# Two graph attention layers on one core: the scaled rows of both layers in half rows that begin at multiples of 16 bytes

## The reference

```python
# layer 0: 8 heads of width 128, x is [4096, 256]
Wh = einsum('nf,hfd->hnd', x, W_heads)
e = leaky_relu(s1[:, :, None] + s2[:, None, :], 0.2)   # s1, s2: Wh with a1, a2
att = softmax(where(adj > 0, e, -9e15), axis=-1)
feat = elu(einsum('hnm,hmd->hnd', att, Wh))            # heads side by side: [4096, 1024]
x = layernorm(x + feat @ W_out + b_out)
# layer 1: 4 heads of width 64
xt = einsum('ni,hio->hno', x, W)
att = softmax(where(adj > 0, leaky_relu(src + dst, 0.2), -inf), axis=2)
x = layernorm(x + heads_side_by_side(att @ xt))
```

## Time and profile before

| | us |
|---|---|
| median of 3 runs | 2743.63 |
| lowest and highest run | 2739.69, 2745.17 |
| span of the profiled execution, first to last instruction | 2745.7 |
| setup and projections | 0 to 191 |
| layer 0's sweeps | 191 to 2045.6 |
| the stage between | 2045.6 to 2232 |
| layer 1's sweeps and the end | 2232 to 2745.7 |

### The profile page before, as it was taken

One profiled execution on the slowest core, in us unless ns is written; L12 is line 12 of the kernel. 1 busy time (PEld: TensorE's weight loads), 2 busy tenths in 40 slices (PEclk: granted clock), 3 DMA queues, 4 the chain that ended last, 5 costly groups with the idle time before them and its releaser, 6 DMA issues.

```text
span 2745.7 us, 62711 instructions
## 1 busy us (share of the span) xinstructions
PE 2674.9 (97%) x26553; PEld 2342.3 (85%) x26553; DVE 1979.0 (72%) x3206; ACT 2071.0 (75%) x3253; POOL 571.0 (21%) x479
## 2 busy tenths in 40 slices
PE   8889999999999999999999999999999999999998
PEld 6558887888888888888888888888888889999998
DVE  6546678777776776777777677675555679989898
ACT  5467877777777777777777777777763669999997
POOL 1220036333222322332322232230002310000000
PEclk9999999999999999999999999999999999999999
DMA  9975421111111110110111111002115555333330
GB/s 342 378 292 183 155 81 43 31 28 35 30 28 27 36 35 26 36 31 28 35 30 28 27 35 35 26 21 55 35 37 165 196 178 189 110 105 110 106 123 17
DMA packets 196384, 240.81 MB, mean 88 GB/s; under 512 B 14853, under 2 KB 125448, under 8 KB 196106
## 3 DMA queue, kind: packets, MB, share of 16 engines
q1 hardware_dynamic: 196106, 236.81, 26.9%
HBM read 178.91 MB, written 57.05 MB: 86 GB/s over the span
## 4 chain that ended last, share of the span: by engine, by line
PE 78%; DVE 9%; ACT 7%; DMA 3%; issue 2%; SPq 0%; POOL 0%; ACTq 0%; DVEq 0%; POOLq 0%
PE l_ps L781 59%; PE l_ps L890 10%; PE l_ps L818 4%; ACT l_arena L1019 3%; DMA l_wh<-l_arena 2%; PE l_ps L748 2%; ACT l_arena L1108 2%; DVE l_arena L1569 1%; DVE l_arena L1568 1%; PE l_ps L843 1%; PE l_ps L806 1%; DVE l_arena L1374 1%; DVE l_arena L1373 1%; DVE l_arena L1577 1%; DVE l_arena L1557 1%
## 5 line engine op out<-in xcount | busy, mean ns | idle before, releaser
L781 PE MATMUL l_ps<-l_arena 128*128 128x258 f16 x16384 | 1833.2, 273 | 7.9 <-DVE l_arena L1374 4.3
L781 PEld LDWEIGHTS l_ps<-l_arena 128*128 128x128 fp8e4 x16384 | 1591.6, 97 | 247.1 <-DVE l_arena L1374 5.7
L1019 ACT ACTIVATE l_arena<-l_arena 128x512 fp8e4<-128x512 f32 x2048 | 1281.5, 708 | 91.2 <-PE l_ps L781 89.2
L1373 DVE SCALAR_TENSOR_TENSOR l_arena<-l_arena,l_mask 128x512 uint32<-128x512 uint32 x512 | 468.1, 914 | 404.4 <-ACT l_arena L1019 401.6
L890 PE MATMUL l_ps<-l_arena 128*128 128x130 f16 x8000 | 475.5, 220 | 19.0 <-DVE l_arena L1577 8.3
L890 PEld LDWEIGHTS l_ps<-l_arena 128*128 128x128 fp8e4 x8000 | 470.0, 98 | 24.4 <-DVE l_arena L1569 19.7
L1374 DVE TENSOR_TENSOR l_arena<-l_arena,l_mask 128x512 uint32<-128x512 uint32 x512 | 488.4, 954 | 0.0
L1108 ACT ACTIVATE l_arena<-l_arena 128x1024 fp8e4<-128x1024 f32 x434 | 457.4, 1141 | 5.1 <-PE l_ps L890 4.7
L405 POOL TENSOR_TENSOR l_arena<-l_arena 128x516 f32<-128x516 f32 x119 | 155.0, 1303 | 1209.0 <-PE l_ps L781 1150.2
L1037 ACT COPY l_arena<-l_ps 128x258 f32<-128x258 f32 x256 | 93.8, 369 | 243.9 <-PE l_ps L781 243.7
L1379 DVE SCALAR_TENSOR_TENSOR l_arena<-l_ps,l_arena 128x258 f32<-128x258 f32 x256 | 117.3, 482 | 146.9 <-ACT l_arena L1037 146.8
(11 more groups left out here) (164 smaller groups left out, 1290.2 us busy)
## 6 DMA issues: line engine op xcount, KB each, us to landing
l_arena<-in_adj SPq DMA_DIRECT2D x128, 512.0 KB, 6.5
l_arena<-uv SPq DMA_DIRECT2D x125, 260.0 KB, 5.5
l_arena<-l_wh SPq DMA_DIRECT2D x64, 256.0 KB, 4.5
l_arena<-l_srow SPq DMA_DIRECT2D x64, 256.0 KB, 3.3
feat<-l_arena SPq DMA_DIRECT2D x64, 256.0 KB, 2.2
l_arena<-feat SPq DMA_DIRECT2D x32, 512.0 KB, 3.7
l_wh<-l_arena SPq DMA_DIRECT2D x64, 192.0 KB, 7.5
uv<-l_arena SPq DMA_DIRECT2D x8, 1040.0 KB, 5.1
```

The costliest lines, as they stand in the source:

```text
L781: last = nc.tensor.matmul(sums(t, m), pattern(k, m).bitcast(F8)[:, j, t * P:(t + 1) * P], uv[:, slot(h, order[k]) + j, 2 * m * W1:2 * (m + ...
L1019: ins = act.activation(pattern(k, 0).bitcast(F8)[:, j, :], s1b[q][:, :], ACT.Relu, bias=kc[:, h, jt:jt + 1], scale=STEEP, saturate=False)
L1373: dve.scalar_tensor_tensor(c, v, ONE8X4, m, ALU.bitwise_xor, ALU.bitwise_and)
```

## The change

The half rows get a pitch of their own. In layer 0 it is `WH = 264` columns or 528 bytes, in layer 1 `VH = 136` columns or 272 bytes, so that every half row starts at a multiple of 16 bytes. The 6 columns behind each half row are read by no matmul and written by none of the engines. The matmuls read as many columns as before. In layer 1 the sums of m = 1 move from column 130 to column 136 of their PSUM bank. DMAs of layer 1's scaled rows carry the gaps too: a chunk becomes 272 KB, a stored stage 1088 KB (1040 before).

`uv` grows by 1248 bytes a partition. The buffers behind it in the arena move up, those of layer 0 by 1248 bytes each but for one that moves by 1120 (`sc`, `kc` and what follows them), and so do those of layer 1, by 1120 to 1536 bytes (a few small ones by another multiple of 16). The arena grows by 1120 bytes, and the area set aside for dynamic DMA descriptors shrinks from 1024 to 256 bytes.

Every queue holds the same instructions in the same order with the same waits.

```diff
+    WH = 264
...
-        arena = s.sb("arena", [P, 96208], U8)
+        arena = s.sb("arena", [P, 97328], U8)
...
-        uv = at(0, F16, 2, (CPB + TWIN) * JC, 4 * W1)
-        bc = at(53664, U8, 1, nbuf, 2, JC * blk)
+        uv = at(0, F16, 2, (CPB + TWIN) * JC, 2 * WH)
+        bc = at(54912, U8, 1, nbuf, 2, JC * blk)
...
-        HD2, V1, W4 = H2 * D2, D2 + 1, 4 * (D2 + 1)
+        HD2, V1, VH, W4 = H2 * D2, D2 + 1, 136, 2 * 136
...
-            return uv[:, slot(h, c):slot(h, c) + JC, j * W1:(j + 1) * W1]
+            first = j // 2 * WH + j % 2 * W1
+            return uv[:, slot(h, c):slot(h, c) + JC, first:first + W1]
...
-            return ps2[:, t, m * 2 * V1:(m + 1) * 2 * V1]
+            return ps2[:, t, m * VH:m * VH + 2 * V1]
...
         def staged(j):
-            return stage[:, :, :, j * V1:j * V1 + D2]
+            first = j // 2 * VH + j % 2 * V1
+            return stage[:, :, :, first:first + D2]
...
-                                                            uv[:, slot(h, order[k]) + j, 2 * m * W1:2 * (m + 1) * W1],
+                                                            uv[:, slot(h, order[k]) + j, m * WH:m * WH + 2 * W1],
...
-                                at = jt * W4 + m * 2 * V1
+                                at = jt * W4 + m * VH
...
-                dve.tensor_scalar(part2[:, :, 2 * V1:], part2[:, :, 2 * V1:], fv.bitcast(F32)[:, c, h:h + 1], None,
+                dve.tensor_scalar(part2[:, :, VH:VH + 2 * V1], part2[:, :, VH:VH + 2 * V1], fv.bitcast(F32)[:, c, h:h + 1], None,
...
-    nc = bacc.Bacc("TRN2", target_bir_lowering=False, num_devices=1, dynamic_dma_scratch_size=1024)
+    nc = bacc.Bacc("TRN2", target_bir_lowering=False, num_devices=1, dynamic_dma_scratch_size=256)
```

More of the change, by code:

```diff
@@ L137, in at @@
             return flat_view
-        uv = at(0, F16, 2, (CPB + TWIN) * JC, 4 * W1)
-        bc = at(53664, U8, 1, nbuf, 2, JC * blk)
[L141 to L149, removed]
+        uv = at(0, F16, 2, (CPB + TWIN) * JC, 2 * WH)
+        bc = at(54912, U8, 1, nbuf, 2, JC * blk)
+        s1b = [at(71296 + q * 2048, F32, 4, blk) for q in range(2)]
+        mnb = [at(75392 + q * 512, F32, 4, D) for q in range(2)]
+        whx = [at(76416 + k * 2064, F32, 4, JC, W1) for k in range(4)]
+        tu, tv = (at(84672 + k * 2064, F32, 4, JC, W1) for k in range(2))
+        eu, ev = (at(88800 + k * 1024, F32, 4, H, NT) for k in range(2))
+        ident16 = at(90848, BF16, 2, P)
+        sc, kc = (at(91104 + k * 1024, F32, 4, H, NT) for k in range(2))
+        e1 = at(93152, F32, 4, TPB, 2 * W1)
+        zr = at(97280, F32, 4, 3, TPB)
         vt, mt, ob = e1[:, :, 0:W1], e1[:, :, W1:W1 + D], e1[:, :, 0:D]
         words = uv[:, :, :].rearrange("p c w -> p (c w)").bitcast(I32)
-        chunk, twin, RAW, PK = JC * 2 * W1, CPB * JC * 2 * W1, 4 * blk, blk
+        chunk, twin, RAW, PK = JC * WH, CPB * JC * WH, 4 * blk, blk
         raws = [words[:, at:at + RAW] for at in (twin, twin + RAW, 4 * chunk, 4 * chunk + RAW)]
@@ L165, in network @@
         slots = bc[:, :, :, :].rearrange("p k m c -> p (k m) c").bitcast(F32)
-        prod = at(75168 + 2064, F32, 4, H, D)
+        prod = at(76416 + 2064, F32, 4, H, D)
         wscore = slots[:, 0:KF, 0:2 * D + C2]
@@ L219, in network @@
         uv2 = at(0, F16, 2, 2, NT * W4)
-        bc2 = at(33280, U8, 1, nbuf2, 2, JC2 * blk2)
+        bc2 = at(34816, U8, 1, nbuf2, 2, JC2 * blk2)
         spare2 = at((G2 % 2) * NT * W4 * 2, U8, 1, 2, 2, JC2 * blk2)
[L222 to L234, removed]
@@ L235, in network @@
-        zr2, lam2, peaks2 = at(95616, F32, 4, TPB2), at(95648, F32, 4, 4), at(95664, F32, 4, H2 + 1)
-        top2, diag2 = at(95684, F32, 4, 1)[0:H2 + 1, :], at(95688, F32, 4, H2 + 1)[0:H2 + 1, :]
+        s1b2 = at(67584, F32, 4, 2, blk2)
+        z = at(76416, F32, 4, TPB2, F)
+        e2 = at(84608, F32, 4, TPB2, 2 * V1)
+        wall2 = at(88768, F32, 4, KF2, HD2 + 2 * H2)
+        st, mv = at(90880, F32, 4, TPB2, 6), at(76288, F32, 4, TPB2, 2)
+        rt, rs = at(76352, F32, 4, TPB2), at(76384, F32, 4, TPB2)
@@ new lines, in network @@
+        scol2 = at(91104, F32, 4, 2, NT * H2).rearrange("p m (t h) -> p m t h", h=H2)
+        eu2, ev2, sc2, kc2, nk, ta2, tb2 = (at(92128 + k * 512, F32, 4, H2, NT) for k in range(7))
+        kall, kt, kmax = at(95712, F32, 4, CPB, H2), at(95840, F32, 4, H2), at(96256, F32, 4, H2)
+        dk, fu1, fv1 = (at(base, F32, 4, CPB, H2) for base in (95872, 96288, 96416))
+        fu, fv = (at(base, I32, 4, CPB, H2) for base in (96000, 96128))
+        units2 = at(75776, F32, 4, P)[0:H2 + 1, :]
+        eps = at(96832, F32, 4, 1)
@@ L238, in network @@
+        zr2, lam2, peaks2 = at(96736, F32, 4, TPB2), at(96768, F32, 4, 4), at(96784, F32, 4, H2 + 1)
+        top2, diag2 = at(96804, F32, 4, 1)[0:H2 + 1, :], at(96808, F32, 4, H2 + 1)[0:H2 + 1, :]
         wo = at(0, F32, 4, KO, F)
         fin = [at(8192 + u * 4096, F32, 4, K) for u in range(2)]
-        stage = at(16640, F16, 2, H2, JC2 * W4).rearrange("p h (t w) -> p h t w", t=JC2)
-        whr = [at(24960 + w * 4096, F32, 4, JC2, HD2) for w in range(2)]
-        scaled = [s1b2[:, 1, :].rearrange("p (t c) -> p t c", t=JC2), at(85408, F32, 4, JC2, HD2)]
@@ L243, in network @@
-        ft = [at(57856 + p * 4096, F32, 4, KO, P) for p in range(2)]
-        xt2 = [at(85408 + p * 1024, F32, 4, KF2, P) for p in range(2)]
-        rows2 = [at(84384 + p * 512, F32, 4, P)[0:JC2 * H2, :] for p in range(2)]
+        stage = at(17408, F16, 2, H2, JC2 * W4).rearrange("p h (t w) -> p h t w", t=JC2)
+        whr = [at(26112 + w * 4096, F32, 4, JC2, HD2) for w in range(2)]
+        scaled = [s1b2[:, 1, :].rearrange("p (t c) -> p t c", t=JC2), at(86656, F32, 4, JC2, HD2)]
+        ft = [at(59392 + p * 4096, F32, 4, KO, P) for p in range(2)]
@@ L246, in network @@
+        xt2 = [at(86656 + p * 1024, F32, 4, KF2, P) for p in range(2)]
+        rows2 = [at(85632 + p * 512, F32, 4, P)[0:JC2 * H2, :] for p in range(2)]
         xin = [z[:, u, :] for u in range(4)]
@@ L362, in staged @@
         def staged(j):
-            return stage[:, :, :, j * V1:j * V1 + D2]
+            first = j // 2 * VH + j % 2 * V1
+            return stage[:, :, :, first:first + D2]
         def stage_one(j):
-            return stage[:, :, :, j * V1 + D2:(j + 1) * V1].rearrange("p h t a -> p h (t a)")
+            first = j // 2 * VH + j % 2 * V1
+            return stage[:, :, :, first + D2:first + V1].rearrange("p h t a -> p h (t a)")
         def turned_rows(c):
```

## The result

The changed kernel takes 2719.07 us (median of 4 runs) against 2744.4: a ratio of 0.9905, 95% interval 0.9894 to 0.9917. It is faster, by 25 us and not by 51, and lies outside the forecast range of 2682 to 2704. The profiled execution spans 2716.8 us, 28.9 less than before.

A forecast was written before the change was run, and what follows sets the result against it. PE, busy 97% of the span, was taken as the bound, with ACT and DVE also near their limit in layer 1. Layer 0 -40 and layer 1 -11 made -51 us, giving 2692.6 us against the 2743.6 median; range 2682 to 2704.

The forecast's parts named there:

- the price of an aligned matmul: Layer 0's sweeps: 12288 of 16384 matmuls start off 16 bytes and each saves 3.37 ns, 41.4 us.
- the gain would be 29 us: Layer 0's lower bound, if aligned matmuls stood 2.3 ns over their columns like the transposes; kept only for the range.
- The first blocks: Layer 0's first blocks, where a faster PE waits longer: 2 or 3 blocks may lose 0.65 us each; 1.4 us taken off.
- Layer 1's cycle: Layer 1's sweeps: 19.8 us on offer, but the cycle between ACT, DVE and PE lets only 11 us arrive.
- the forecast's split by blocks: Four layer 1 blocks: two give 0.86 us each, one about 1.1, the ACT and DVE one 0.2; 3.0 us together.
- Moved buffers: All moves are by multiples of 16 bytes, so no other operand changes its place within 16 bytes: 0 us.
- The larger DMAs: Layer 1's chunks and stored stages grow 4.6% but are fetched a block ahead: 0 us, or 2 us without that cover.
- only a part of layer 0's gain comes (29 us): Rival: layer 0 gains only 29 us, or aligned reads meet a stall; 2703 to 2720 us, 5%.
- The short distance belongs to the matmul that comes next: Rival: a matmul is cheap only when starting 4 bytes past the previous one's line; slower, to 2764 us, 3%.
- The rival by lines: Rival: price goes by 16-byte lines an operand touches, equal for all starts; time stays 2743.6 us, 4%.

The follow-up runs named there:

- 192-column run: The changed kernel with matmuls in blocks 1 to 7 of layer 0 reading and writing 192 of 258 columns; 0.9895 of the kernel before.
- moved_only: The changed kernel with buffers moved and descriptor area shrunk, but rows without gaps in both layers; 1.0002 of the kernel before.
- order_both: The kernel before, no gaps, with another order of the 8 matmuls of a chunk and tile in both layers; 2718.27 us, 0.9899 of before.
- after_again: The changed kernel measured once more, beside order_both on one chip; 2718.62 us, 0.99 of the kernel before.
- alt08: The changed kernel with layer 0's halves 536 bytes apart, row pitch 1056, so starts alternate 0 and 8 bytes past a multiple of 16; 2717 to 2721 us.
- cols256: The changed kernel with layer 0's matmuls reading 256 of 258 columns, two of the sums' columns left out; 109.2 ns a matmul.
- alt04: The changed kernel with layer 0's second half 516 bytes on, row pitch 1056, so starts alternate 0 and 4 bytes past a multiple of 16; 2728.86 us.

## Why the prediction was wrong

**The step that failed** is the price of an aligned matmul: "Each saves 112.5 - 109.2 = 3.37 ns". The sorting was right and the reading of it was not. The 109.2 ns were one of four distances in a repeating pattern, which the start of the matmul, the start of the next and the end of the last all explained equally well. I took the cheap one as the price of a uniform layout. Measured, a uniform layout has 110.0, and three of four distances of before carry a price for sharing. The cheap distance is 4 clocks over its columns beside dear ones of 12, and in the changed layout every distance is 6 over. On offer were 16384 x (111.71 - 110.0) = 28.0 us and not 41.4, and in layer 1 8192 x (58.41 - 56.70) = 14.0 and not 19.8. The number was in the text as a bound: the transposes of the earlier trace rows are pairs of aligned operands at 2.3 ns over their columns, "the gain would be 29 us". I set them aside as another operation; they were the nearer case, because they had the step between starts that the change makes.

**The first blocks** were the second miss: I gave 1.4 us for them. Of the 28.0 us on offer, blocks 9 to 63 could give 24.1 and gave 22.1: in six blocks (15, 23 and each eighth to 55) PE now also waits 0.3 us for DVE's patterns, at a time when POOL makes rows. There DVE is slow: its masking operation (L1378, 512 of them) takes 0.68 us where POOL is idle and 1.53 us in the median where POOL works during nearly all of it. Blocks 0 to 8, where 3.9 was on offer, became 1.2 us longer, for two reasons. Blocks 0 to 7 took 249.3 us in place of 249.9: in blocks 1 to 7 the chain over ACT and DVE leaves PE slack, as the 192-column run shows. Block 8 took 33.5 us in place of 31.7, because TensorE's clock fell there (see the last section). This also happens without the gaps, and the one profile of the kernel before happens not to have it, so these 1.8 us are a chance of the profiles and no cost of the change. The sign of the slack stood in the earlier trace rows, where PE waited for evacuations in 5 places: I took those waits as small losses beside PE's work, when they mark blocks that PE does not bound at all.

**Layer 1's cycle** was right where it was read, with the wrong price, but it does not hold for the blocks as I had sorted them. Rows 8 and 9 show block 11, counted from 0, and not block 10 as they say. The same block after the change, ACT in order of time:

```profile
2552.90 0.59 ACT L1126 COPY l_arena<-l_ps 128x520 f32<-128x520 f32 x1 [0.80 <-PE l_ps L894]
...
2555.95 26.11 ACT L1112 ACTIVATE l_arena<-l_arena 128x1024 fp8e4<-128x1024 f32 x25
2582.85 0.59 ACT L1126 COPY l_arena<-l_ps 128x520 f32<-128x520 f32 x1 [0.80 <-PE l_ps L894]
```

The wait before the copy was 1.40 and is 0.80. The 356 matmuls of that path at 1.71 ns saved are 0.61 us. Block 11 went from 30.56 to 29.96 us, which is this 0.61. But block 10, of the same length and kind before, gave only 0.10 (30.46), and so did blocks 6 and 14: PE saves its 0.87 us there and waits 0.77 us longer, 0.5 of it at the block's end, where it had not waited before. Block 8, which I had called ACT's and DVE's own, gave 0.5 and block 9 gave 0.9. Together blocks 8 to 11 take 122.1 us where they took 124.1. (The four blocks of the earlier trace rows add up to 124.2 us and not 124.3, which changes nothing.) So the forecast's split by blocks was wrong and its sum fared better: of 19.8 us I let 56% through; of 14.0, 7.8 came, also 56%. That the shares are the same is luck. In the profiles of the other runs with layer 1's gaps its sweeps take 497.2 to 500.3 us, most of the spread in the first block and in each second of four. No run took ACT's or DVE's work out of layer 1, so what the cycle holds back is read from the trace and not shown by a run.

**The rest.** Moved buffers at 0: right, shown by moved_only. The larger DMAs at 0: right too, since order_both has none of them and takes 2718.27 us beside after_again's 2718.62. In the profile after, a chunk of 272 KB still lands in 5.5 us, and a stored stage of 1088 KB in 5.2 (5.1 before). Of the rivals, "only a part of layer 0's gain comes (29 us)" is the one that happened, and I had given it 5%. "The short distance belongs to the matmul that comes next" had the right doubt, that the records could not tell which of two matmuls pays; its outcome, slower, did not come. The rival by lines is refuted as a forecast, since the time fell. Its premise that the count of lines (33) is the same for all four places stays true: with 33 lines each, a matmul took 264 to 268 clocks in the mean. The Trainium skill, "SBUF — State Buffer", section "Specifications (TRN2)", speaks of a penalty for each crossing to a new 16-byte line; what these runs show is a price where the next operand starts in the line in which the last one ended.

## What to carry to other kernels

Where a rate alternates in a pattern, the cheapest of its distances is not the price of a uniform layout: look for a place in the same trace, even of another operation, that already has the step from one instruction to the next that the change will make, and price by the mean. Where matmuls in a stream read neighbouring pieces, as the f16 operands do here, see that none begins in the 16 bytes in which the last one ended; here another loop order did it with no padding. And small waits of the busiest engine can mark stretches that another engine bounds: give such a stretch no gain until its chain has been followed.

## What the runs showed of the hardware that I had not expected

A matmul here costs its columns plus 6 clocks in the mean at 252, 256, 258 and 130 columns, with single distances from 4 to 14 over in layouts without sharing; in alt08 they make up for each other exactly.

DVE's masking operation takes over twice its time beside a working POOL: 1.53 us against 0.68 for the same 128x512 operation, as said above.

The clock can fall for a few microseconds behind a short pause in the middle of a busy program. In block 8 PE waits 2.6 to 3.2 us for POOL's first rows. Before, it went on at 1.00; in the changed kernel it ran at 0.51, the lower level of 1.2 GHz, for 3 us and 16 matmuls stood 214 ns apart. First before, then after:

```profile
467.00:470.00 3.00, 3.00 (x30) 2.61 (x28) 0.64 (x2) 0.75 (x2) 0.00 (x0) 1.00 0.48 155
```

```profile
467.00:470.00 3.00, 3.00 (x16) 2.12 (x15) 0.49 (x1) 0.38 (x1) 0.00 (x0) 0.51 0.41 136
```

It is not the gaps that do it: moved_only, which has none, shows 0.50 at 464 to 468 us, and its block 8 takes 34.5 us. Nor is it the length of the pause: 2.96 us in before and 2.97 in moved_only. Of the 20 profiles of this case 17 show the fall, with a block 8 of 33.0 to 34.5 us, and three do not (before 31.7, cols256 31.7, alt04 31.6). What decides whether it falls stays open. In the changed kernel it costs 16 x (214 - 110) ns = 1.7 us, in moved_only 2.8.

```profile
464.00:468.00 4.00, 3.02 (x15) 2.16 (x16) 1.34 (x2) 0.61 (x1) 0.83 (x1) 0.50 0.43 124
```
